# Stops moved between lanes on VectorE, later token stores and additions in a gated mixture-of-experts block

## The reference

```python
def _align_one(small, large):
    D = _pairwise_euclidean(small, large)
    R = _dtw_cost(D)
    i_idx, j_idx, valid = _backtrack(R, T_small, T_large)
    contrib = small[i_idx] * valid[:, None].astype(small.dtype)
    expanded = jnp.zeros((T_large, d), dtype=small.dtype).at[j_idx].add(contrib)
    return expanded
...
logits = xf @ gate_w.T
w, sel = jax.lax.top_k(logits, TOP_K)
w = jax.nn.softmax(w.astype(jnp.float32), axis=1).astype(xf.dtype)
...
expert_out = jnp.einsum('nc,edc->ned', xf, expert_w)
out = jnp.einsum('ne,ned->nd', w_full, expert_out)
...
x = x + jnp.tanh(g_xattn[0]) * _L0_xattn_ref(ctx_1024, _layernorm(x, axis=-1))
x = x + jnp.tanh(g_ffn[0]) * _L0_ffn_ref(_layernorm(x, axis=-1), L0_ffn_gate_w, L0_ffn_expert_w)
```

## Time and profile before

| | |
|---|---|
| median of three runs | 565.06 us (564.70 to 566.52) |
| the profiled execution | 566.38 us |
| its span in the profile | 564.6 us |
| busy: TensorE, VectorE | 430.5 us (76%), 463.3 us (82%) |
| busy: ScalarE, GpSimd | 240.5 us (43%), 218.7 us (39%) |

### The profile page before, as it was taken

How to read it: one execution, slowest core, us unless ns; L and a number is a source line. 1 busy time by engine, 2 the same in 40 slices (tenths; PEclk the granted TensorE clock), 3 DMA queues, 4 the chain that set the end, 5 groups by cost and what they waited for, 6 DMA issues and landing times.

```text
span 564.6 us, 7995 instructions
## 1 busy us (share of the span) xinstructions
PE 430.5 (76%) x1818; PEld 249.5 (44%) x1829; DVE 463.3 (82%) x1970; ACT 240.5 (43%) x461; POOL 218.7 (39%) x214
## 2 busy tenths in 40 slices
PE   8999943557512230368799979999999999999991
PEld 8989832435411220134444634444444444444440
DVE  6868889999998888589989839999987997798900
ACT  5447788774565520299557122222222222222210
POOL 4470213000000000000325276768677867688652
PEclk9999976676856565679799989999999999999997
DMA  8966244452007400177599997679797979699775
GB/s 284 340 217 209 78 117 112 120 140 71 1 0 268 180 2 0 44 280 278 186 304 331 273 224 176 130 136 165 135 163 135 164 133 161 127 165 164 118 91 73
DMA packets 61243, 88.88 MB, mean 157 GB/s; under 512 B 24917, under 2 KB 24917, under 8 KB 61037
## 3 DMA queue, kind: packets, MB, share of 16 engines
q0 software_dynamic: 15904, 37.31, 36.4%
q1 hardware_dynamic: 38701, 42.64, 23.2%
q10 hardware_dynamic: 6592, 8.42, 4.8%
HBM read 48.92 MB, written 39.43 MB: 156 GB/s over the span
## 4 chain that ended last, share of the span: by engine, by line
PE 36%; DVE 29%; DMA 22%; issue 5%; POOL 3%; ACT 2%; SPq 1%; POOLq 0%; ACTq 0%; DVEq 0%
PE psum L2057 25%; DMA out_dram<-tokens,row_ids 7%; DVE met L1048 6%; DMA out_dram<-prow,row_ids 5%; DVE waves L962 5%; PE psum L1788 4%; DMA dist_rows<-work 3%; DVE tokens L1051 3%; DVE tokens L986 3%; DVE shf L953 2%; DVE tokens L965 2%; DMA stage<-x_rows,row_ids 2%; DMA out_dram<-tokens 2%; DVE tokens L956 2%; DMA x_rows<-st 2%
## 5 line engine op out<-in xcount | busy, mean ns | idle before, releaser
L2057 PE MATMUL psum<-big,tokens 128*128 x304 | 132.6, 592 | 0.0
L761 POOL DMA_INDIRECT stage<-x_rows,row_ids x57 | 56.2, 987 | 196.4 <-DVE row_ids L1230 177.3
L2057 PE MATMUL psum<-big,work 128*128 x264 | 119.1, 602 | 0.0
L1385 DVE STREAM_TRANSPOSE tokens<-stage 32x256 f32<-32x256 f32 x192 | 83.7, 436 | 16.4 <-DMA stage<-x_rows,row_ids 12.8
L1385 DVE STREAM_TRANSPOSE work<-stage 32x256 f32<-32x256 f32 x192 | 83.7, 436 | 7.5 <-DMA stage<-x_rows,row_ids 5.0
L2057 PEld LDWEIGHTS psum<-big,tokens 128*128 128x128 f32 x304 | 57.1, 190 | 68.9 <-issue 68.9
L780 POOL DMA_INDIRECT out_dram<-tokens,row_ids x36 | 58.2, 1616 | 47.6 <-DMA out_dram<-tokens 15.5
L2057 PEld LDWEIGHTS psum<-big,work 128*128 128x128 f32 x264 | 50.0, 194 | 58.1 <-issue 58.1
L1713 ACT ACTIVATE prow<-psum,tile_shares 128x512 f32<-128x512 f32 x35 | 24.1, 687 | 95.2 <-PE psum L2057 65.2
L1713 ACT ACTIVATE tokens<-psum,tile_shares 128x512 f32<-128x512 f32 x36 | 24.6, 686 | 93.2 <-PE psum L2057 65.4
L780 POOL DMA_INDIRECT out_dram<-prow,row_ids x35 | 55.9, 1597 | 20.7 <-issue 7.6
(11 more groups left out here) (392 smaller groups left out, 693.1 us busy)
## 6 DMA issues: line engine op xcount, KB each, us to landing
tokens<-in_x_dram SPq DMA_DIRECT2D x16, 1024.0 KB, 12.5
stage<-in_L_ffn_expert_w_dram ACTq DMA_DIRECT2D x8, 1024.0 KB, 5.6
out_dram<-tokens SPq DMA_DIRECT2D x8, 1024.0 KB, 10.4
x_rows<-tokens SPq DMA_DIRECT2D x7, 1024.0 KB, 7.0
tokens<-dist_rows SPq DMA_DIRECT2D x52, 64.0 KB, 2.1
dist_rows<-work SPq DMA_DIRECT2D x16, 160.0 KB, 2.0
dist_rows<-prow SPq DMA_DIRECT2D x5, 256.0 KB, 10.1
x_rows<-tokens SPq DMA_DIRECT2D x4, 256.0 KB, 4.5
```

The source lines that it names most:

```text
L761: pool.indirect_dma_start(out=tiles_in(n)[:, 0, :], out_offset=None, in_=x1_d[0:T, :] if n < FA else x1_d[:, :], in_offset=bass.IndirectOf ...
L1385: ins = v.transpose(to[:, :, :, NB * g:NB * (g + 1)], got[:, :, :, a, :])
L2057: ins = nc.tensor.matmul(psum[:, UP + n % UP, :], tileT(n, c), expT[:, bass.ds(own, 1), c, :].rearrange("p o d -> p (o d)"), start=(c == 0 ...
```

## The change

- The stops no longer go through DRAM. Each lane keeps its stops in `turns`, and shifts them by its number in five conditional steps, of 16, 8, 4, 2 and 1 places: a step takes the shifted value times a bit of the lane's number plus the unshifted one times its complement. The last step writes `stopr`. The bits are made in `lane_columns`.
- 10 warm-up matmuls instead of 14.
- SyncE stores the second batch's tokens after the gathers of tiles 9 to 11 have landed.
- `LAG` is 3 at tile 11, 4 at 12, 5 from 13 to 23, 4 to 29, 3 to 35, and 2 elsewhere. `AHEAD` reaches nine tiles ahead from round 12 instead of 18.
- TensorE transposes tile 9 behind the matmuls of tile 8.

```diff
@@ -85,7 +85,9 @@
     UY = 8
     UP = 2
     DEPTH = 3
-    LAG = [min(n, 2, NSEQ - 1 - n) for n in range(NSEQ)]
+    LATER = {FA + 2: 3, FA + 3: 4, **{n: 5 for n in range(FA + 4, FA + 15)}, **{n: 4 for n in range(FA + 15, FA + 21)},
+             **{n: 3 for n in range(FA + 21, FA + 27)}}
+    LAG = [min(n, LATER.get(n, 2), NSEQ - 1 - n) for n in range(NSEQ)]
     PARTS = 3
     LAST = E + 1
     G = E + 1
@@ -94,7 +96,6 @@
 
     x1_d = nc.dram_tensor("x1_rows", (B * T, RW), F32, kind="Internal").ap()
     dist_d = nc.dram_tensor("dist_rows", (ROWS, T), F32, kind="Internal").ap()
-    stop_d = nc.dram_tensor("stops", (P, NS), F32, kind="Internal").ap()
 
     with ExitStack() as ctx:
         def sb(name, shape, dt=F32):
@@ -160,11 +161,12 @@
         cgx = sb("ctx_gate", [P, B, G])
         cgr = sb("ctx_gate_rest", [SR3, B, G])
         gmean = sb("gate_means", [P, 1])[64:64 + E, :]
-        stops = flat[:, half + (2 * NS + 1) * TW // 2:half + (2 * NS + 1) * TW // 2 + NS]
         gw = prow[64:64 + E, :].bitcast(F32)[:, 0:C]
         cgT = flat[0:G, dlo + DR * CS * W1:dlo + DR * CS * W1 + B * (SM + SR3)].rearrange("p (b r) -> p b r", b=B)
-        assert B * (SM + SR3) <= C and dlo + DR * CS * W1 + C <= half and (2 * NS + 1) * TW // 2 + NS <= half
+        assert B * (SM + SR3) <= C and dlo + DR * CS * W1 + C <= half
         side = sb("side", [P, B])
+        bits = sb("lane_bits", [P, 5], U32)
+        moved = sb("lane_moved", [P, 2, 5])
         ends = sb("ends", [P, 2, 2, B])
         limits = sb("row_limits", [P, 2, 2, 2, B])
         HT = T // 2
@@ -208,6 +210,7 @@
         xgs = sb("x_gate", [P, NT, E])
         work = sb("work", [P, 4, GW])
         tmpq = work[:, 2, 0:3 * NS].rearrange("p (k s) -> p k s", k=3)
+        turns = work[:, 3, 0:4 * NS].rearrange("p (k s) -> p k s", k=4)
         offspan = work[:, 0:2, :].rearrange("p k c -> p (k c)")
         held = work[:, 2:4, :].rearrange("p k c -> p (k c)").bitcast(F16).rearrange("p (k c) -> p k c", k=2)
         stopr = work[:, 0:2, :].rearrange("p k c -> p (k c)")[:, 0:2 * (P + 160)].rearrange("p (k r) -> p k r", k=2)
@@ -372,8 +375,6 @@
         s_next = sem("neighbour_word")
         s_fill = sem("entries_filled")
         s_stop = sem("stops_by_step")
-        s_so = sem("stops_out")
-        s_si = sem("stops_in")
         s_sr = sem("stops_by_row")
         s_end = sem("row_ends")
         s_p = sem("path_cells")
@@ -559,14 +560,6 @@
             for g in range(GB):
                 sp.dma_start(x[:, GT * g:GT * g + GT, :], x_v[g]).then_inc(s_x[g], 16)
             sp.wait_ge(s_stop, 2)
-            sp.dma_start(stop_d[:, :], stops[:, :]).then_inc(s_so, 16)
-            sp.wait_ge(s_so, 16)
-            for h in range(2):
-                for b in range(B):
-                    q = (2 * h + b) * NB
-                    at = stop_d[q:q + 1, 0 if h else NB - 1:NS]
-                    sp.dma_start(stopr[q:q + NB, 0, h * H:(h + 1) * H],
-                                 bass.AP(at.tensor, at.offset, [[NS + 1 if h else NS - 1, NB], [1, H]])).then_inc(s_si, 16)
             for g in range(GB, NG):
                 sp.dma_start(x[:, GT * g:GT * g + GT, :], x_v[g]).then_inc(s_x[g], 16)
 
@@ -591,6 +584,8 @@
             for n in range(FA - UX, FA):
                 sp.wait_ge(s_xi[n % UX], 16 * (n // UX + 1))
             sp.dma_start(x1_d[0:T, C:RW].rearrange("(t p) k -> p t k", p=P), pairs[:, 0:TB, :]).then_inc(s_sto[0], 16)
+            for n in range(FA, FA + 3):
+                sp.wait_ge(*landed(n))
             for g in range(GB, NG):
                 tokens_out(g)
 
@@ -783,7 +778,7 @@
                 ).then_inc(s_add[n % DEPTH], 16)
 
             AHEAD = [n + UX for n in range(FA - UX + 1)] + [FA + 2, FA + 3, FA + 5]
-            AHEAD += [min(n + min(9, 6 + (n - FA) // 3), NSEQ) for n in range(FA, NSEQ + 1)]
+            AHEAD += [min(n + min(9, 6 + n - FA), NSEQ) for n in range(FA, NSEQ + 1)]
             for n in range(UX):
                 gather(n)
             added = 0
@@ -926,6 +921,13 @@
                 link(v.tensor_scalar(blk, blk, -float(W), float(W * (NB - 1)), ALU.mult, ALU.add))
                 link(v.tensor_scalar(offs, blk, -2.0, None, ALU.add))
                 link(v.scalar_tensor_tensor(offs, offs, sign, offj, ALU.mult, ALU.add))
+                for k in range(5):
+                    ins = v.tensor_scalar(bits[:, k:k + 1], lanei[:, 1:2], k, 1, ALU.logical_shift_right, ALU.bitwise_and)
+                link(ins)
+                link(v.tensor_copy(moved[:, 0, :], bits[:, :]))
+                link(v.tensor_scalar(moved[:, 0, :], moved[:, 0, :], -1.0, 0.5, ALU.mult, ALU.add))
+                link(v.tensor_scalar(moved[:, 0, :], moved[:, 0, :], sign, 0.5, ALU.mult, ALU.add))
+                v.tensor_scalar(moved[:, 1, :], moved[:, 0, :], -1.0, 1.0, ALU.mult, ALU.add)
                 v.memset(codes[:, 0:1], 0.0)
                 link(v.tensor_scalar(codes[:, 1:W1 + 1], counting[:, :], CODE, size, ALU.add, ALU.mult))
                 link(v.tensor_scalar(col2[:, :], counting[:, 0:W], blk, 2.0, ALU.add, ALU.mult))
@@ -1056,14 +1058,31 @@
             v.tensor_scalar(ok, y, 0.0, None, ALU.is_gt)
             link(v.tensor_scalar(z, y, sign, offs, ALU.mult, ALU.add))
             link(v.scalar_tensor_tensor(ok, y, float(W1), ok, ALU.is_le, ALU.mult))
-            v.tensor_tensor(stops[0:P // 2, :], z[0:P // 2, :], ok[0:P // 2, :], ALU.mult).then_inc(s_stop, 1)
-            v.tensor_tensor(stops[P // 2:P, :][:, ::-1], z[P // 2:P, :], ok[P // 2:P, :], ALU.mult).then_inc(s_stop, 1)
-
             hi = slice(P // 2, P)
-            v.wait_ge(s_si, 16 * 2 * B)
-            v.tensor_copy(stopr[hl, 1, 0:H - 1], stopr[hl, 0, 1:H])
+            got, kept = turns[:, 0, :], turns[:, 2, :]
+            v.tensor_tensor(got[hl, :], z[hl, :], ok[hl, :], ALU.mult).then_inc(s_stop, 1)
+            v.tensor_tensor(got[hi, :][:, ::-1], z[hi, :], ok[hi, :], ALU.mult).then_inc(s_stop, 1)
+            v.wait_ge(s_stop, 2)
+            width = NS
+            for k in (4, 3, 2, 1):
+                width -= 1 << k
+                to = turns[:, 1 if k % 2 else 3, :]
+                link(v.tensor_scalar(kept[:, 0:width], got[:, 0:width], moved[:, 1, k:k + 1], None, ALU.mult))
+                link(v.scalar_tensor_tensor(to[:, 0:width], got[:, 1 << k:(1 << k) + width], moved[:, 0, k:k + 1],
+                                            kept[:, 0:width], ALU.mult, ALU.add))
+                got = to
+            link(v.tensor_scalar(kept[:, 0:H], got[:, 0:H], moved[:, 1, 0:1], None, ALU.mult))
+
+
+            def settled(rows, k, to, at, n):
+                return v.scalar_tensor_tensor(stopr[rows, k, to:to + n], got[rows, at + 1:at + 1 + n], moved[rows, 0, 0:1],
+                                              kept[rows, at:at + n], ALU.mult, ALU.add)
+
+            settled(hl, 0, 0, 0, H)
+            settled(hl, 1, 0, 1, H - 1)
             v.tensor_copy(stopr[hl, 1, H - 1:H], jcol[hl, :])
-            v.tensor_copy(stopr[hi, 1, H + 1:S], stopr[hi, 0, H:S - 1])
+            settled(hi, 0, H, 0, H)
+            settled(hi, 1, H + 1, 0, H - 1)
             link(v.tensor_copy(stopr[hi, 1, H:H + 1], jcol[hi, :]))
             for k in range(2):
                 ins = v.tensor_copy(stopr[:, k, 160:160 + SR3].rearrange("p (j r) -> p j r", j=3)[:, :, 0:SR],
@@ -1911,7 +1930,7 @@
             pe.wait_ge(s_ctxv, 11)
             pe.wait_ge(s_wc, CH * E)
             pe.wait_ge(s_stop, 2)
-            for _ in range(14):
+            for _ in range(10):
                 nc.tensor.matmul(psum[:, 0, :], sm[:, 0, 0, 0:P], sm[:, 0, 0, 0:C], start=True, stop=True)
             pe.wait_ge(s_sr, 1)
             for a, at in enumerate((0, 160)):
@@ -2062,9 +2081,11 @@
             turn(0)
             for n in range(NSEQ):
                 own = owned(n)
-                if n + 1 < NSEQ:
+                if n + 1 != FA and n + 1 < NSEQ:
                     turn(n + 1)
                 expert(n, own)
+                if n + 1 == FA:
+                    turn(FA)
                 if n == 0:
                     count()
                 if n == 1:
```

## The result

| | before | after |
|---|---|---|
| median of six runs each | 565.79 us | 572.72 us (571.50 to 574.47) |
| ratio, 95% interval | | 1.0114 (1.0091 to 1.0138) |
| span of the profiled execution | 564.6 us | 570.1 us |
| TensorE, tile 12 starts | 345.2 us | 349.2 us |
| last addition starts | 554.60 us | 560.13 us |

A forecast was written before the change was run, and what follows sets the result against it. TensorE was taken to bound the expert stage, gated by VectorE's block 12/13, with GpSimd's additions nearly level. TensorE's +2.8 us less 0.8 swallowed gave +2.0 on the 565.06 us median: 567.1 us, range 563.3 to 569.5.

The forecast's parts named there:

- What bounds the kernel, and where the hole goes: Expert stage: VectorE's block 12/13 gates TensorE; the 3.54 us hole ahead of tile 8 becomes 6.4 us ahead of tile 12.
- The price of a gather under the stores: Gather 13 under the held stores: 6.2 us instead of 3.9, so 2.3 us more.
- The bound of 4 us more: Upper bound for gather 13 under the stores, with three additions queued ahead and shared engines: 4 us more than 3.9.
- The fall of the clock: TensorE's tiles after the hole ahead of tile 12: the granted clock falls and costs 1.7 us more.
- The 0.8 us that the additions' lateness was to swallow: Kernel's end: additions already 0.8 us later than TensorE's work asks absorb that much of TensorE's +2.8, leaving +2.0.
- The additions' own queue: GpSimd's additions chain with the new lags and gathers ahead: +0.9 us (0 to 2), not counted since TensorE's is later.
- The wait of addition 12: GpSimd, flagged addition 12: waits about 3.0 us with its gathers already issued, so 1.45 us lost.
- Stops and lane bits: Ahead of the second list: exchange on VectorE gains 1.3 us, lane bits lose 1.0; together -0.3 us (-1.1 to +0.2).
- Light sharing: Rival: gathers lose only 0.65 us to the stores, the additions chain's +0.9 decides, 566.0 us; chance 0.28.
- Kept gains: Rival: lane bits hide, exchange gives 1.6 us, gather 13 keeps 3.9 us and lands before 336; 563.2 us; chance 0.17.
- Additions that run into the stores and the buffers: Rival: addition 12 lands over 7 us late, ScalarE's copy of tile 20 and TensorE wait; 5 us or more, 570; chance 0.10.

The follow-up runs named there:

- The part alone: Kernel before with only TensorE's transposes of tile 9 moved behind the matmuls of tile 8: ratio 1.0011 to the kernel before.
- the stops alone: Kernel before with only the stops moved on VectorE, lane bits in the early stage and ten warm-up matmuls: ratio 0.9985.
- stores held alone: Kernel before with only the second batch's token stores made to wait for gathers 9 to 11: ratio 1.0135.
- the better order: Kernel before with tile 9's transposes behind tile 8 and gathers 12 and 13 ahead of additions 5 to 7, stores as before: ratio 0.9983.
- the lags alone: Kernel before with only the change's `LAG` and `AHEAD`, additions up to five tiles behind and gathers ahead sooner: ratio 1.0045.
- all three held kernels: The changed kernel (1.0114), the kernel before with only the stores held (1.0135), and the changed kernel with half of the stores early (1.0117).
- three variants: Kernel before with only stores held (1.0135); changed kernel with stores behind five gathers (1.0153); that with gathers 12 and 13 first (1.0131).
- two other kernels with the stores held: Changed kernel with two of four token stores early (1.0117), and kernel before with only the stores held (1.0135).
- the stores behind five gathers: Changed kernel with the second batch's token stores held behind the gathers of tiles 9 to 13 instead of three gathers: ratio 1.0153.
- stores early: Changed kernel with SyncE storing the second batch's tokens as before, without waiting for gathers 9 to 11: ratio 1.0033.

## Why the prediction was wrong in size

- **What bounds the kernel, and where the hole goes.** Right. The hole ahead of tile 8 went, one opened ahead of tile 12, ended by VectorE's block. The part alone gained nothing (1.0011).
- **The price of a gather under the stores.** This step failed. I took 6.2 us for gather 13, 2.3 more than before, from three gathers said to be the same transfer under the same stores. They weren't: their packets moved only when the stores ran out, and no addition stood ahead of them. The bound of 4 us more, 7.9 us in all, was too low as well. Measured are 9.0, 8.7 and 8.2 us. In place of the 6.2, the traces show GpSimd's queue standing for some 3 us when the stores began and then getting about half of the engines' time for what was queued. That is 2.8 us beyond my term, and it went to the end one for one.
- **The fall of the clock.** 1.7 us forecast; 12.09 less 10.46 is 1.6. In other runs a fall cost from 1.0 us (tile 8 with the stops alone) to 2.9 us (stores held alone), so the closeness is in part luck.
- **The 0.8 us that the additions' lateness was to swallow.** Wrong. After, the last addition is 1.0 us behind its data, as before. I took the lateness for a full queue's. I now read it as the wait of the last additions for the landing of those before them (by the code addition n waits for addition n - 3 to land; before, the last but one waited 1.61 us for such a landing), which moves with the data; that is argued from the rows, not shown. With TensorE 2.2 us sooner it grew to 2.4 us (the better order), so the queue was full only just below the old point. TensorE's 2.8 + 2.8 us came through whole: 558.46 against 552.85, 5.6 us, and the last addition 5.5 us later.
- **The additions' own queue.** +0.9 forecast (0 to 2); the lags alone gave +1.7 by the last addition and 2.5 us by the ratio. The wait of addition 12 was nearly right (2.72 of 3.0), the wait of the gathers for their buffer's shares was short.
- **Stops and lane bits.** -0.3 us forecast, -0.8 by the ratio (-1.5 to -0.2). Both terms were right in kind: 0.88 for 1.0 lost, 1.06 for 1.3 gained. That fewer warm-ups put the row of limits at half clock, I had not seen: 0.2 to 0.8 us. I had put the last two of the ten at full clock; all ran at 0.50, and they ended with VectorE's moves and not ahead of them.
- **The rivals.** Light sharing would have shown gather 13 at 4.6 us, 566.0 us: refuted by all three held kernels. Kept gains asked for a gather 13 before 336 us: it landed at 341.86. Additions that run into the stores and the buffers were priced at 570 us, nearest to what was measured, but addition 9 waited only 1.26 us in the changed kernel; in three variants it waited 8.6 to 10.4 us for the stores.

In sum 2.0 us became 5.5 in the trace: 2.8 from the gather, 0.8 from the swallow that wasn't, less 0.1 of rest; the remaining 0.9 us to the 6.4 of the ratio lies within its interval (5.1 to 7.8).

## What to carry to other kernels

A large store that isn't urgent costs least in a stretch where the DMA engines have nothing that anybody waits for; look at the DMA share of the stretch that it leaves and of the one that it enters. Before a hole ahead of the matmuls is closed, ask which producer is next and how much slack it has: here 0.3 us, so that 5 us of visible waste were worth nothing. Before a transfer is priced by its like "under the same load", look at each queue's packets: whether it moved beside that load or waited for it to end. And count what is queued ahead of it on its own queue.

## What the runs showed of the hardware that I had not expected

- While stores from SyncE's queue moved, GpSimd's indirect DMAs were off the engines for about 3 us (share 104 and 107% for q1 and none for q0 at 331 to 333 us of the kernel after; the same in two other kernels with the stores held), and only then the queues shared. In the kernel before they were off them from 323 to 326 us, until the stores ran out. It isn't so each time: with the stores behind five gathers, which began at 340 us, q0 had 22.1% from 341 to 346 us. The Trainium skill (DMA: Bandwidth & Descriptors, Queues, rings and completion order) says that an engine takes turns between its queues by packets. The later microseconds agree with that (77 packets of each queue from 343 to 344 us, 83 of each in the next). The first three don't, if a packet of the profile, 2 KB here, is a turn; the page lets a turn hold up to 64 descriptors, and whether the profile's packets are these no run shows.
- The length of a hole doesn't tell whether TensorE's clock falls: after 3.15 us tiles 12 and 13 took 7.13 us at a granted clock of 1.00 (tile 9 turned behind 8), after 2.90 us three tiles took 12.26 instead of 10.46 us, with 0.77 granted from 342.7 to 350 us (stores early).
